# Expert stage of a decoder layer: the two-unit lag runs on across heads, next head's work in 16 steps

## What is computed

```python
q = einsum('bnd,de->bne', x, w_q)                       # 2 x 8 x 128 columns
q = (q - mean) * rsqrt(var + BN_EPS) * gamma + beta     # over all 1792 tokens
sim = einsum('pbnhd,hkpd->pbnhk', q, keys)              # 2 halves, 8 heads, 128 keys
sx, ix = top_k(sim[0], 8); sy, iy = top_k(sim[1], 8)
scores, pk = top_k(sx[..., :, None] + sy[..., None, :], 8)     # over 64 pairs
indices = take_along_axis(ix * 128 + iy, pk)            # 8 experts of 16384
h = gelu_new(einsum('bnd,bnhkd->bnhk', x, down_embed[indices]))
out = einsum('bnhk,bnhkd->bnd', softmax(scores) * h, up_embed[indices])
```

## Time and profile before

| | |
|---|---|
| Time, median of 3 runs | 3729.27 us (3718.15 to 3739.54) |
| Profiled execution: span from first to last instruction | 3638.0 us |
| Around the span: the median less the span | 91.3 us |
| PE busy, granted clock over the span | 3112.1 us, 0.921 |
| DVE, ACT, POOL busy | 2057.4, 1229.3, 1123.6 us |
| Experts chosen for head 0: from 2178.3 to 2251.5 | 73.2 us |
| Gathers: first to last | 2252.8 to 3616.4 us |
| Moved by the gathers | 469.8 MB in 896 |

### The profile page before, as it was taken

How to read it: one execution, slowest core, us unless ns; L and a number is a source line. 1 busy time by engine, 2 the same in 40 slices (tenths; PEclk the granted TensorE clock), 3 DMA queues, 4 the chain that set the end, 5 groups by cost and what they waited for, 6 DMA issues and landing times. The chain is left out here.

```text
span 3638.0 us, 43572 instructions
## 1 busy us (share of the span) xinstructions
PE 3112.1 (86%) x12584; PEld 1803.2 (50%) x12584; DVE 2057.4 (57%) x5970; ACT 1229.3 (34%) x3110; POOL 1123.6 (31%) x1100
## 2 busy tenths in 40 slices
PE   7899899899999998998998955878787878888777
PEld 4574574564665665664755733434343434333323
DVE  3553654544544545545545534667676767676855
ACT  2353343343334333433423521323232323222322
POOL 2001002002001001011011011666666666666765
PEclk9999999999999999999999967889898989898889
DMA  3000000000000000000000012989898989898998
GB/s 136 18 1 11 18 2 11 18 7 6 18 12 1 18 12 1 18 12 7 12 6 1 1 53 84 362 331 349 335 356 340 360 334 358 312 365 319 357 358 342
DMA packets 156968, 514.81 MB, mean 142 GB/s; under 512 B 16848, under 2 KB 27088, under 8 KB 156720
## 3 DMA queue, kind: packets, MB, share of 16 engines
q0 software_dynamic: 129024, 469.82, 33.9%
q1 hardware_dynamic: 24192, 36.95, 3.0%
q10 hardware_dynamic: 3504, 5.19, 0.5%
HBM read 504.56 MB, written 7.34 MB: 141 GB/s over the span
## 5 line engine op out<-in xcount | busy, mean ns | idle before, releaser
L1195 PE MATMUL e_ps_out<-e_rows,e_diag 128*128 128x512 f32 x1792 | 869.3, 644 | 232.5 <-ACT e_diag L1393 232.5
L1150 POOL DMA_INDIRECT e_rows<-in_experts,e_idx x896 | 911.2, 1017 | 447.2 <-issue 252.2
L1326 DVE CUSTOM_DVE_ANT_0 e_rows<-e_rows,xn_all 128x512 f32<-128x512 f32 x896 | 580.9, 689 | 264.0 <-DMA e_rows<-in_experts,e_idx 262.0
L1195 PEld LDWEIGHTS e_ps_out<-e_rows,e_diag 128*128 128x128 f32 x1792 | 365.7, 208 | 717.4 <-issue 447.0
L826 POOL TENSOR_TENSOR rstd<-var_eps,minus_half 112x2 f32<-112x2 f32 x16 | 11.5, 719 | 1353.9 <-DVE var_eps L505 1353.9
L1393 ACT ACTIVATE e_diag<-ident_f,e_weight 128x128 f32<-128x128 f32 x896 | 278.2, 390 | 437.8 <-DVE e_weight L1305 262.2
L679 DVE SCALAR_TENSOR_TENSOR neg_s<-ps_s,mask 112x750 f32<-112x750 f32 x256 | 240.4, 939 | 309.0 <-PE ps_s L438 309.0
L438 PE MATMUL ps_s<-k_t,q_m 128*112 128x375 f32 x1024 | 396.9, 513 | 16.1 <-DVE q_m L669 16.1
L458 PE MATMUL ps_o<-prob_t,v_c 125*32 125x112 f32 x3072 | 338.0, 261 | 0.0
L782 ACT ACTIVATE prob<-neg_s,neg_max 112x750 f32<-112x750 f32 x256 | 235.6, 920 | 292.5 <-DVE neg_max L689 292.5
L458 PEld LDWEIGHTS ps_o<-prob_t,v_c 125*32 125x32 f32 x3072 | 278.1, 110 | 26.7
(11 more groups left out here) (163 smaller groups left out, 3386.8 us busy)
## 6 DMA issues: line engine op xcount, KB each, us to landing
e_rows<-in_experts,e_idx POOLq DMA_INDIRECT x896, 6.3
ctx_t<-in_ctx_t SPq DMA_DIRECT2D x8, 1500.0 KB, 6.5
e_w_q<-in_ffn_wq SPq DMA_DIRECT2D x16, 256.0 KB, 4.9
x_in<-in_x SPq DMA_DIRECT2D x8, 448.0 KB, 3.7
x_dram<-x ACTq DMA_DIRECT2D x8, 448.0 KB, 3.2
out<-acc SPq DMA_DIRECT2D x14, 256.0 KB, 5.8
w_qkv<-in_w_qkv_t SPq DMA_DIRECT2D x1, 3072.0 KB, 21.2
acc<-x_dram SPq DMA_DIRECT2D x1, 3072.0 KB, 11.3
```

What stands on the lines that cost most here:

```text
L1150: pool.indirect_dma_start(rows[:, v % RING, k, :], None, table[:, :], bass.IndirectOffsetOnAxis(ap=idx[:, e:e + 1], axis=0))\
L1195: mm = nc.tensor.matmul(ps_out[t % 2][:], diag[:, k, :], rows[:, v % RING, k % HU, D:], start=(k == 0), stop=(k == TOP - 1))
L1326: nc.vector.tensor_tensor_reduce(down, down, xn_all[:, t, :], 1.0, 0.0, ALU.mult, ALU.add, hidden[:, s, k:k + 1])
```

## The change

- Every engine's unit loop no longer ends with a head. `before(h, t, n)` gives the unit n earlier, across the boundary; weights and add_rows of a head's last units are done inside units 0 and 1 of the next head, finish is left for the end of all heads. The loop over heads runs from unit 2 to unit 1 of the next head.
- PE does weigh_rows first and its step behind it.
- The next head's choosing is cut in 16 steps of one chunk or one group of four tiles, which start four units earlier (LEAD = 4): step k of head h + 1 comes in unit k - 4, and steps 0 to 3 of head h + 2 in units 10 to 13.
- DVE's affine is parted in count (statistics of one chunk) and affine, ACT's in root and affine, a unit apart.
- Search reads the similarities in PSUM; ACT's copy is gone, and PE waits for searched in place of sims_ready.
- choice handles both halves in one operation of 1792 elements instead of two of 896.
- GELU is one ScalarE operation, Gelu_apprx_tanh; DVE's cubic pair and one of two operations in weights are gone. ACT loads tables 23 times in the program's text instead of 14.
- POOL's and SP's programs are as before.

The diff, cut to what the next section speaks of (semaphores, buffers and renamed counters are left out):

```diff
-        PE_STEPS = {0: [("project", 0, 0)], 1: [("project", 0, 1)], 3: [("match", 0, 0)],
-                    4: [("match", 0, 1), ("project", 1, 0)], 5: [("project", 1, 1)], 7: [("match", 1, 0)],
-                    8: [("match", 1, 1)]}
-        ACT_STEPS = {2: [("affine", 0, 0)], 3: [("match", 0, 0)], 4: [("match", 0, 1)], 6: [("affine", 1, 0)],
-                     7: [("match", 1, 0)], 8: [("match", 1, 1)], 10: [("soften", 0, 0)]}
-        DVE_STEPS = {2: [("affine", 0, 0)], 4: [("search", 0, 0)], 5: [("search", 0, 1)], 6: [("affine", 1, 0)],
-                     8: [("search", 1, 0)], 9: [("search", 1, 1)], 10: [("pairs", 0, 0)], 11: [("choice", 0, 0)]}
-        N_STEPS = 12
-
-        def run_heads(eng, steps, start, unit, finish):
+        PE_STEPS = {**{c: [("project", 0, c)] for c in range(QC)},
+                    **{6 + c: [("project", 1, c), ("match", 0, c)] for c in range(QC)},
+                    12: [("match", 1, 0), ("match", 1, 1)], 13: [("match", 1, 2), ("match", 1, 3)]}
+        DVE_STEPS = {1: [("count", 0, 0)], 2: [("count", 0, 1)], 3: [("count", 0, 2)], 4: [("count", 0, 3)],
+                     5: [("affine", 0, 0)],
+                     7: [("search", 0, 0), ("count", 1, 0)], 8: [("search", 0, 1), ("count", 1, 1)],
+                     9: [("search", 0, 2), ("count", 1, 2)], 10: [("search", 0, 3), ("count", 1, 3)],
+                     11: [("affine", 1, 0)],
+                     13: [("search", 1, 0), ("search", 1, 1)],
+                     14: [("search", 1, 2), ("search", 1, 3), ("pairs", 0, 0)], 15: [("choice", 0, 0)]}
+        ACT_STEPS = {4: [("root", 0, 0)], 5: [("affine", 0, 0)], 10: [("root", 1, 0)], 11: [("affine", 1, 0)],
+                     14: [("soften", 0, 0)]}
+        N_STEPS = 16
+        LEAD = 4
...
+        def opening(h, t):
+            return isinstance(h, int) and NTF * h + t < 0
+
+        def before(h, t, n):
+
+            return (h, t - n) if t >= n else (h - 1, t - n + NTF)
+
+        def nth_unit(h, t):
+            return NTF * h + t
+
+        def run_heads(steps, unit, finish, eng):
+
+            def worked(h, t, next_one=True, next_but_one=True):
+                unit(h, t)
+                if next_one and t + LEAD < N_STEPS:
+                    steps(h + 1, t + LEAD)
+                if next_but_one and t >= NTF - LEAD:
+                    steps(h + 2, t - NTF + LEAD)

             for k in range(N_STEPS):
                 steps(0, k)
-            with eng.Fori(0, HF - 1) as h:
-                start(h)
-                for t in range(NTF):
-                    unit(h, t, lambda: steps(h + 1, t))
-                finish(h)
-            start(HF - 1)
+            for k in range(LEAD):
+                steps(1, k)
+            for t in range(2):
+                worked(0, t)
+            with eng.Fori(0, HF - 2) as h:
+                for t in range(2, NTF):
+                    worked(h, t)
+                for t in range(2):
+                    worked(h + 1, t)
+            for t in range(2, NTF):
+                worked(HF - 2, t, next_but_one=False)
             for t in range(NTF):
-                unit(HF - 1, t, lambda: None)
-            finish(HF - 1)
+                worked(HF - 1, t, next_one=False, next_but_one=False)
+            finish()
...
-            def unit(h, t, step):
-                step()
-                if t >= 1:
-                    weigh_rows(h, t - 1)
-
-
             pe.sem_inc(rows_used, RING)
-            run_heads(pe, steps, lambda h: None, unit, lambda h: weigh_rows(h, NTF - 1))
+            run_heads(steps, lambda h, t: weigh_rows(*before(h, t, 1)), lambda: weigh_rows(HF - 1, NTF - 1), pe)
...
+            def count(head, half, c):
+                dve.wait_ge(q_done, QC * nth(head, half) + c + 1)
+                nc.vector.bn_stats(stats[:, c, :], ps_q[c][:, 0:QN])
+                if c == QC - 1:
+                    nc.vector.drain()
+                    nc.vector.bn_aggr(mean_var[:], stats[:].rearrange("p c n -> p (c n)"))
+                    nc.vector.drain()
+                    nc.vector.tensor_scalar(var_eps[:], mean_var[:, 1:2], BN_EPS, None, ALU.add).then_inc(bn_var, 1)
+
...
+            def search(head, half, g):
+
+                dve.wait_ge(sims_made, NG * nth(head, half) + g + 1)
                 dve.sem_inc(passed_dve, 1)
-                tiles = [*group(2 * part), *group(2 * part + 1)]
-                for i in tiles:
-                    nc.vector.max(best[:, half, i, :], q_t[:, i * NK:(i + 1) * NK])
-                nc.vector.drain()
-                for i in tiles:
-                    last = nc.vector.max_index(best_at[:, half, i, :], best[:, half, i, :], q_t[:, i * NK:(i + 1) * NK])
-                if part == 1:
-                    last.then_inc(searched, 1)
+
+                def sims(i):
+                    return ps_m[g % 2][:, (i % TPB) * NK:(i % TPB + 1) * NK]
+
+                for i in group(g):
+                    nc.vector.max(best[:, half, i, :], sims(i))
+                nc.vector.drain()
+                for i in group(g):
+                    last = nc.vector.max_index(best_at[:, half, i, :], best[:, half, i, :], sims(i))
+                last.then_inc(searched, 1)
...
-                for half in range(2):
-                    nc.vector.drain()
-                    nc.vector.tensor_tensor(match.rearrange("p t k j -> p (t k) j"), spread(at_f[:, half, :], 2, TOP),
-                                            spread(eight[:], 1, PICK), ALU.is_equal)
-                    nc.vector.drain()
-                    nc.vector.tensor_tensor(match, match, spread(best_at_f[:, half], 2, TOP), ALU.mult)
-                    nc.vector.drain()
-                    nc.vector.tensor_reduce(chosen[:, half, :], match.rearrange("p t k j -> p (t k) j"), AX_X,
-                                            ALU.add)
+                nc.vector.drain()
+                found = match.rearrange("p t k j -> p (t k) j")
+                nc.vector.tensor_tensor(found, spread(at_f[:].rearrange("p s n -> p (s n)"), 2, TOP),
+                                        spread(eight[:], 1, 2 * PICK), ALU.is_equal)
+                nc.vector.drain()
+                nc.vector.tensor_tensor(match, match, spread(best_at_f[:].rearrange("p s t j -> p (s t) j"), 2, TOP),
+                                        ALU.mult)
+                nc.vector.drain()
+                nc.vector.tensor_reduce(chosen[:].rearrange("p s n -> p (s n)"), found, AX_X, ALU.add)
...
+                dve.wait_ge(active_ready, nth_unit(h, t) + 1)
+                nc.vector.tensor_tensor(weight[:, s, :], active[:, s, :], gate[:, t * TOP:(t + 1) * TOP], ALU.mult)\
+                    .then_inc(weight_ready, 1)
...
-                    if k == 1 and t >= 1:
-                        weights(h, t - 1)
-                    if k == HU and t >= 2:
-                        add_rows(h, t - 2)
-                nc.vector.drain()
-
-                nc.vector.scalar_tensor_tensor(cubic[:, s, :], hidden[:, s, :], 0.044715, hidden[:, s, :],
-                                               ALU.mult, ALU.mult)
-                nc.vector.drain()
-                nc.vector.scalar_tensor_tensor(cubic[:, s, :], cubic[:, s, :], 1.0, hidden[:, s, :], ALU.add,
-                                               ALU.mult).then_inc(cubic_ready, 1)
-                step()
-
-            def finish(h):
-                weights(h, NTF - 1)
+                    last = nc.vector.tensor_tensor_reduce(down, down, xn_all[:, t, :], 1.0, 0.0, ALU.mult, ALU.add,
+                                                          hidden[:, s, k:k + 1])
+                    if k == 1:
+                        weights(*before(h, t, 1))
+                        if t == 0:
+                            nc.vector.drain()
+                            nc.vector.tensor_copy(gate[:], gate_next[:])
+                            nc.vector.drain()
+                    if k == HU:
+                        add_rows(*before(h, t, 2))
+                last.then_inc(hidden_ready, 1)
...
-            def match_out(head, half, part):
-                n = nth(head, half)
-                for g in (2 * part, 2 * part + 1):
-                    act.wait_ge(sims_made, NG * n + g + 1)
-                    tiles = group(g)
-                    nc.scalar.copy(q_t[:, tiles[0] * NK:(tiles[-1] + 1) * NK], ps_m[g % 2][:, 0:len(tiles) * NK])\
-                        .then_inc(sims_ready, 1)
-
...
+            def unit(h, t):
+                diagonals(*before(h, t, 1))
+                act.wait_ge(hidden_ready, nth_unit(h, t) + 1)
+                nc.scalar.activation(active[:, t % 2, :], hidden[:, t % 2, :], ACT.Gelu_apprx_tanh)\
+                    .then_inc(active_ready, 1)
+
+            run_heads(steps, unit, lambda: diagonals(HF - 1, NTF - 1), act)
```

122 lines of the change are left out of this document (51 added, 71 removed).

## The result

The changed kernel takes 3775.7 us (median of 4 runs, 3755.3 to 3790.0) against 3734.4 (3718.2 to 3742.5): a ratio of 1.0108, 95% interval 1.0064 to 1.0153. Five more rounds gave 1.0118 (1.0098 to 1.0139). It is slower by 1.1%, 41 to 44 us. The forecast of 3738 was too low by 38; the range held the time.

The account below looks back on a forecast made before the run. DMA was taken as the floor, with POOL's waits for PE all that could be won. Terms −79 + 17 + 0 + 60 − 6 − 1 + 18 = +9, added to the median 3729.27, gave 3738 us, range 3695 to 3790.

Parts of the forecast that it names:

- DMA is the floor: Expert stage: POOL's 896 gathers at unhindered pace take 1206 of 1363.6 us; only waits for PE can be won.
- Not all of a wait is lost: POOL's waits for row buffers: queued gathers run on, so 157 of 194 us are lost, a factor of 0.81.
- The 91.3 us lie around the span: Whole run: the median 3729.27 us exceeds the profiled span by 91.3 us, taken as time outside the span.
- Mid-head −79: POOL's mid-head waits for PE go, as row work comes first and PE's units take 10.9 us: −79 us (−97 to −40).
- PE's clock at the boundary: PE after idling at head boundaries: granted clock drops, slowing unit 13 and once more per head; +18 us (0 to +30).
- Half 26 +17: POOL's wait before half 26: DVE's two searches ahead of pairs delay unit 11 by 2.4 us, +17 us (0 to +30).
- Half 2 +60: New POOL wait before half 2: unit 13's weights come after half 0 lands; 8.6 us per boundary, +60 (+40 to +70).
- GELU at nothing: DVE's units: one-operation GELU saves 0.7 us each, spent waiting for rows; 0, and −1 us at the tail.
- PSUM search and table loads at nothing: DVE's search reading PSUM costs nothing more; ACT's some 16 extra table loads lie in its waits for DVE: 0.
- rival (c): DVE's search: PSUM reads cost 66 ns more per instruction, +9 us, 3747 us in all; chance 0.05.
- (a): Head boundary: half 2 finds its slot free and the mid-head gain stands alone, 3678 us; chance 0.15.
- (b): Mid-head: PE's clock drops, units start late and never catch up, half the gain is lost, 3789 us; chance 0.18.

Follow-up runs that it names:

- lead5: Changed kernel with the pairs in a step of their own (17 steps, LEAD 5): ratio 1.0036 to the kernel before, 31 us below the changed kernel.
- weights13: Changed kernel with DVE making unit 13's weights at the end of unit 13, not in the next head's unit 0: 3741.9 us, ratio 1.0011 to the kernel before.
- the ring: Kernel before, heads written out, with row-buffer slots running on across heads, so POOL looks six halves ahead everywhere: ratio 0.985 to the kernel before.

## Why the prediction was right or wrong, step by step

The range held the time, but in part by luck. The forecast was no change; the kernel is 1.1% slower, and the 38 us by which it was off are the remainder of some 86 too low and 53 too high (sum below).

- **"DMA is the floor": not shown.** In the last head POOL never waits for PE, and its 112 gathers of 1.04 us with 0.30 us between them give the 150.8 us by themselves. They land a median of 6.5 us after issue and 7.1 at the end, and the queue doesn't grow, with a DMA share of 1.01. So the pace is that of POOL's issuing, and DMA, though full, keeps up.
- **"Not all of a wait is lost" (0.81): wrong.** POOL's idle time is lost in full between the first and the last gather. The 194.1 hold some 10 us of ordinary 0.30 us steps, and the last head, by which the 157 were reckoned, has slower gathers than the others (116.1 us against 113.6 in the mean). For the same reason "the remaining 97.5 in mid-head" are 86.5.
- **"The 91.3 us lie around the span": wrong.** 2 us do. The forecast's sum was made on a quick execution with 184 us of POOL's idle; the second has 280, and of the 96 between them 62 are late signals. Comparing the spans (3638.0, 3753.2) would give +115 us, where the runs give +41.
- **Mid-head −79: the mechanism right, the price wrong.** This is the step that failed most. The waits for PE's work before halves 3 to 25 did go, from 106.4 to 12.7 us. The reason given holds too: PE does units 2, 3 and 4 with their steps in 10.8 us each (2681.97, 2692.74, 2703.50). But late signals there grew from 63.2 to 124.7 us, so that all idle of halves 3 to 25 fell by 32 us only, from 169.6 to 137.5. The quick execution had 0.9 us of late signals, and the sum gave them no term. Kernels in which POOL waits over 100 us for PE's work in mid-head have 63 to 68 us of late signals, the others 116 to 141; that is consistent with a wait for the work hiding the lateness of the signal. What makes the signals late stays open.
- **PE's clock at the boundary: as foreseen, and oftener.** PE's timeline of the changed kernel's first profile (units 13, 0 and 1):

```profile
2622.30 8.76 PE L1219 MATMUL e_ps_out<-e_rows,e_diag 128*128 128x512 f32 x16 [5.81 <-ACT e_diag L1405]
2640.11 10.09 PE L1219 MATMUL e_ps_out<-e_rows,e_diag 128*128 128x512 f32 x16 [9.05 <-ACT e_diag L1405]
2654.57 9.69 PE L1219 MATMUL e_ps_out<-e_rows,e_diag 128*128 128x512 f32 x16 [4.37 <-issue]
```

Each idle of 4 to 9 us is followed by a unit of 8.8 to 10.1 us instead of 7.03. The windows of the same stretch (busy time of each engine, then the granted clock, DMA share, GB/s) show it:

```profile
2640.00:2650.00 10.00, 9.89 (x16) 4.04 (x16) 4.47 (x17) 5.82 (x14) 7.86 (x8) 0.70 1.02 408
...
2654.00:2664.00 10.00, 9.44 (x16) 4.09 (x17) 6.89 (x22) 3.93 (x13) 5.02 (x6) 0.71 0.91 356
2664.00:2690.00 26.00, 25.69 (x81) 13.29 (x79) 15.57 (x59) 4.32 (x15) 17.59 (x18) 1.00 0.94 343
```

  0.70 is a mixture of 1.2 and 2.4 GHz; in the third stretch, with PE busy 25.69 of 26 us, it is 1.00. The prediction had the slow unit 13, and one more drop per head. Over the stage the slower level adds up to 392 us in the kernel before (second profile) and 430 in the changed one; POOL hardly waits for PE behind the boundary.
- **Half 26 +17: right in kind, wrong in size.** The step foresaw 2.4 us more of DVE work behind unit 10, and undisturbed it is 9.4 − 6.8 = 2.6. What it didn't see is that DVE is held up there, by 8 to 11 us in six heads of the second profile and by some 9 in two of the first. Idle before halves 26 and 27: +60 us between the second profiles; in time, by lead5, up to 31.
- **Half 0, no change: right.** 81.3 and 81.4 us.
- **Half 2 +60: the mechanism right, to the place.** 8.6 us per boundary was forecast, 62.1 over seven is 8.9. Charged in full it was too dear: 40 to 43 us by weights13.
- **GELU at nothing: wrong.** Taking its operations out gave 33 us on the kernel before. The step asked only what DVE does with the 0.7 us saved; 20.5 us stand in POOL's gathers, which are shorter.
- **Lead −6: right.** The first gather starts at 2246.55, in the kernel before at 2251.98: 5.4 us.
- **PSUM search and table loads at nothing: no run speaks against it.** The lines of MAX8, changed kernel and kernel before, both second profile:

```profile
L1260 DVE MAX8 e_best<-e_ps_m 128x8 f32<-128x128 f32 x224 | 50.3, 283 | 56.8 <-remote 40.2 <-PE e_ps_m L1202 16.6
```

```profile
L1239 DVE MAX8 e_best<-e_q_t 128x8 f32<-128x128 f32 x224 | 46.5, 281 | 14.0 <-ACT e_q_t L1371 14.0
```

  283 against 281 ns for one; the busy time, in which overlapping instructions count once, grew by 3.8 us for all 224, 17 ns each, while they now come in groups of two to four and not of eight and six. The 65 ns more that the Trainium skill gives ("VectorE: DVE Perf Modes", TRN2 errata) are not seen, and rival (c) falls.
- **Not in the sum: the loop.** Written-out heads are 22 us faster. The kernel before has a loop too, and its own written-out form was run only together with the ring, so how much of this the change added stays open.
- **The rivals.** (a), a bridged boundary, is excluded by 62 us of waits. (b) has the right time (3789) and the right sign, and by the prediction's own test, idle at 10 to 14, it would stand. But its mechanism isn't there: PE isn't behind with that work, as half 14 above shows (of 137.5 us before halves 3 to 25, 12.7 are waits for it), and the last head, which has no steps, has 6.2 us of it before halves 3 to 14 too.

The sum with what was measured: −33 (GELU) + 40 (half 2) + 31 (half 26) − 5 (lead) = +33, and +44 was measured. It takes GELU's gain on the kernel before as good in the changed one, and lead5's as half 26's; neither is shown, though gathers are 18 us shorter in the changed kernel too. The 11 us between are left for the loop (at most +22), mid-head with its late signals, and PE together; they weren't separated. The prediction had −79 + 18 = −61 there, 72 too low, and half 26 14 too low; GELU's missed gain of 33 and half 2's 20 too much took back part of it.

## What to carry to other kernels

A ring that starts anew with each round of a loop shortens its own look-ahead at the seam unless the round is a multiple of its length; count at the seam how many pieces ahead the producer may go, and which work frees each slot. Work that is put off across the seam makes such a shortage worse (half 2, 40 us). Before a sum is made on one profiled execution, see that its span fits the runs: 85 us of difference was a different execution, not something around it. And before an idle is called a wait, look up when the thing waited for was done: the name in the brackets is inferred, and over a third of POOL's idle in the changed kernel came after it.

## What the runs showed of the hardware

- DVE pauses without a wait: up to 8.4 us, between short instructions that depend on nothing outside DVE, in every profile but the first of the kernel before (which has them, over 0.4 us, only behind the loop's branch). They strike often where short instructions stand close together (pairs, search, and in the kernel before behind the drain in weights), which is consistent with half 26.
- PE's signals come late at POOL: by up to 10 us behind the product that they report. They hold POOL idle for up to 4.9 us at a time, 63 to 141 us in all, in every profile but that same first one (0.9).
- The profiles in which both occur are also the ones whose semaphore records are incomplete ("remote" among the releasers); that first one had complete records. What makes them wasn't found, and no run tells whether an execution without the profiler has them.
- When POOL waits for PE's work and the signal is on time, its gather starts 0.8 us after PE's last product ends: 41 of 41 waits in the first profile of the kernel before.
- DVE stands still for about 6 us behind a loop's closing branch: L1316 in the kernel before, 36.9 us in 6 times. There it lies inside the wait for rows.
- POOL's gathers are not of one length: 0.94 us beside an idle DVE, 1.06 in the mean beside its products (second profile of the kernel before). Taking 62.1 us of waits before half 2 away was worth 40 us in time; the rest came back as longer gathers and idle elsewhere.
